# A cap of three gathers in flight in a fused graph layer on one core

## The reference, cut to what matters

```python
# x (12500, 64) f32, src and dst (400000,) int32, dst sorted, edge_attr_64 (400000, 64) f32
msg = x[src] + edge_attr_64
agg = segment_sum(msg, dst, num_segments=12500)
h = relu(agg @ W1 + b1)
x = layernorm(x + h @ W2 + b2, eps=1e-5)
```

## Time and profile before

| what | value |
|---|---|
| median of 3 runs | 2372.08 us |
| profiled execution: its own time | 2373.34 us |
| its span from first to last instruction | 2371.5 us |
| PE busy | 1501.9 us, 63% |
| DVE busy | 1234.8 us, 52% |
| POOL busy | 968.9 us, 41% |
| ACT busy | 738.2 us, 31% |
| gathers (line 610) on POOL | 925, 889.4 us busy |
| mean granted clock of PE | 0.738 |

### The profile page before, as it was taken

How to read it: one execution, slowest core, us unless ns; L and a number is a source line. 1 busy time by engine, 2 the same in 40 slices (tenths; PEclk the granted TensorE clock), 3 DMA queues, 4 the chain that set the end, 5 groups by cost and what they waited for, 6 DMA issues and landing times.

```text
span 2371.5 us, 45768 instructions
## 1 busy us (share of the span) xinstructions
PE 1501.9 (63%) x18752; PEld 1318.1 (56%) x18753; DVE 1234.8 (52%) x2701; ACT 738.2 (31%) x935; POOL 968.9 (41%) x1045
## 2 busy tenths in 40 slices
PE   2555656566657576666566676555756666657776
PEld 1555545455646566656555665455655565546664
DVE  4765545555546355645545554434545554445535
ACT  5322111122223233323222343323433333323323
POOL 7644454443443433443433434343244334243432
PEclk6556776776777767777767777777878777778798
DMA  7322222222212222222222222221222222212232
GB/s 188 75 78 78 76 71 71 61 71 63 79 50 76 68 65 66 69 67 69 69 55 61 73 61 64 54 57 50 69 62 53 61 61 63 59 50 63 69 64 55
DMA packets 150052, 161.03 MB, mean 68 GB/s; under 512 B 42291, under 2 KB 134035, under 8 KB 149507
## 3 DMA queue, kind: packets, MB, share of 16 engines
q1 hardware_dynamic: 118229, 123.61, 18.0%
q0 software_dynamic: 31616, 34.50, 7.5%
HBM read 153.06 MB, written 4.93 MB: 67 GB/s over the span
## 4 chain that ended last, share of the span: by engine, by line
PE 48%; another core or an unknown queue 21%; issue 16%; ACT 8%; DVE 4%; POOL 1%; DMA 1%; DVEq 0%; POOLq 0%; SPq 0%; ACTq 0%
PE sums_ps L1155 18%; PE counted_ps L1138 16%; PE chunk_ps L1120 13%; ACT counts L721 7%; DVE oh_key L937 1%; DVE oh_lo L933 1%; POOL xmsg L610 1%; PE turn_ps L1166 1%; POOL x_parts L659 0%; PE turn_ps L1091 0%; DVE counts L946 0%; DMA lists<-in_src 0%; DMA records<-edge_records,run_at 0%; DVE lists L902 0%
## 5 line engine op out<-in xcount | busy, mean ns | idle before, releaser
L610 POOL DMA_INDIRECT xmsg<-in_x,idx_t x925 | 889.4, 961 | 922.8 <-PE chunk_ps L1120 634.6
L721 ACT CAST counts<-counted_ps 128x784 bf16<-128x784 f32 (+2 forms) x728 | 615.5, 864 | 1385.8 <-remote 667.0
L1138 PE MATMUL counted_ps<-oh_key,oh_lo 128*128 128x98 bf16 (+1 forms) x5264 | 677.8, 257 | 582.1 <-ACT counts L721 335.1
L933 DVE TENSOR_TENSOR oh_lo<-chunk_ps,tables 128x768 bf16<-128x768 f16 (+3 forms) x622 | 446.2, 717 | 764.5 <-remote 359.9
L1138 PEld LDWEIGHTS counted_ps<-oh_key,oh_lo 128*128 128x128 bf16 x5264 | 437.7, 115 | 683.7 <-issue 351.0
L1155 PE MATMUL sums_ps<-x_parts,counts 128*128 128x193 bf16 (+3 forms) x4900 | 749.3, 284 | 56.6 <-issue 55.8
L1155 PEld LDWEIGHTS sums_ps<-x_parts,counts 128*128 128x128 bf16 (+3 forms) x4900 | 542.4, 136 | 74.5 <-issue 64.5
L937 DVE TENSOR_TENSOR oh_key<-chunk_ps,tables 128x1176 bf16<-128x1176 f16 (+2 forms) x622 | 459.9, 739 | 0.0
L1120 PE MATMUL chunk_ps<-onehot,cmsg 128*64 128x16 f32 (+4 forms) x4400 | 227.2, 241 | 116.1 <-issue 115.5
L1120 PEld LDWEIGHTS chunk_ps<-onehot,cmsg 128*64 128x64 f32 x4400 | 206.4, 173 | 146.7 <-issue 141.0
L619 POOL DMA_INDIRECT records<-edge_records,run_at x42 | 39.6, 944 | 394.4 <-DVE run_at L827 371.3
(11 more groups left out here) (111 smaller groups left out, 446.4 us busy)
## 6 DMA issues: line engine op xcount, KB each, us to landing
cmsg<-in_edge_attr SPq DMA_DIRECT2D x440, 160.0 KB
gmsg<-in_edge_attr SPq DMA_DIRECT2D x185, 160.0 KB
xmsg<-in_x,idx_t POOLq DMA_INDIRECT x925
out_nodes<-x_parts SPq DMA_DIRECT2D x11, 256.0 KB, 2.6
edge_records<-counts SPq DMA_DIRECT2D x1, 1500.0 KB
lists<-in_src SPq DMA_DIRECT2D x1, 1400.0 KB
lists<-in_dst SPq DMA_DIRECT2D x1, 1400.0 KB
records<-edge_records,run_at POOLq DMA_INDIRECT x42
```

What stands on the lines that cost most here:

```text
L610: pool.indirect_dma_start(xmsg[:, at * D:(at + 1) * D], None, x, bass.IndirectOffsetOnAxis(ap=idx_t[:, of:of + 1], axis=0)).then_inc(gathe ...
L721: nc.scalar.copy(to.rearrange("p h (m n) -> p h m n", m=m), ps.rearrange("p m (n h) -> p h m n", h=HI)).then_inc(unit_kept, 1)
L933: nc.vector.tensor_tensor(oh_lo[s % RING][:, 0:n * P].rearrange("p (k n o) -> p k n o", k=n, o=2), lo_ps.rearrange("p (n o) -> p n o", o=2 ...
L1138: mm = nc.tensor.matmul(unit_ps[u][:, col:col + slot.key_cols], oh_lo[s % RING][:, n * P:(n + 1) * P], oh_key[s % RING][:, n * slot.key_co ...
```

## The change: three semaphores in turn

Gathers are numbered q = 5k + j through the whole kernel. Gather q waits on POOL until gather q - 3 has landed, and raises semaphore q mod 3. PE waits, for each gathered chunk, on all three semaphores, each for the last of its gathers up to the chunk's end.

```diff
+IN_FLIGHT = 3
...
-        gathered = [sem(f"gathered{s}") for s in range(XSLOTS)]
+        landed = [sem(f"landed{f}") for f in range(IN_FLIGHT)]
...
                 if j == 0 and k >= XSLOTS:
                     pool.wait_ge(summed, PLACE["gather", k - XSLOTS] + 1)
+                q = k * TILES + j
+                if q >= IN_FLIGHT:
+                    pool.wait_ge(landed[q % IN_FLIGHT], 16 * (q // IN_FLIGHT))
                 at, of = t * TILES + j, k * TILES + j
                 pool.indirect_dma_start(xmsg[:, at * D:(at + 1) * D], None, x,
                                         bass.IndirectOffsetOnAxis(ap=idx_t[:, of:of + 1], axis=0)
-                                        ).then_inc(gathered[t], 16)
+                                        ).then_inc(landed[q % IN_FLIGHT], 16)
...
                 pe.wait_ge(gin[s], 16 * (i // GSLOTS + 1))
-                pe.wait_ge(gathered[t], 16 * TILES * (i // XSLOTS + 1))
+                last = i * TILES + TILES - 1
+                for f in range(IN_FLIGHT):
+                    pe.wait_ge(landed[f], 16 * ((last - f) // IN_FLIGHT + 1))
```

## The result

The changed kernel takes **2349.0 us** (median of 4 runs, 2330.4 to 2353.5) against 2372.2 for the kernel before beside it: a ratio of 0.990, with a 95% interval of 0.987 to 0.993. A second comparison gave 0.9905 (0.9875 to 0.9935). The forecast was 2378, no change. The profiled execution is the longest of the four, 2353.5 us; its span is 2351.7.

A forecast was written before the change was run, and what follows sets the result against it. PE was taken to bound the kernel, with POOL's gathers ahead of it except at the start. +4 us (start) and +2 (PE's waits) on the profiled 2373.3 gave 2379.3, or 2378 against the median; range 2362 to 2396.

The forecast's parts named there:

- The reading of the bound: Whole kernel: PE is busiest, 1501.9 of 2371.5 us, and in the long middle the gathers are ahead of it.
- PE's waits: On PE before gathered pairs: 370 more waits, none blocking, cost +2 us, bounds 0 and 18.5.
- POOL's slack: Mid-kernel: POOL waits 1006 us for PE and DVE, so slowing it under 1.09 us per gather costs nothing.
- The start: POOL's first gathers: the cap delays the first records that DVE awaits, +4 us, bounds 0 and +13.6.
- L = 6.0: At the start: assumed us from a gather's beginning to its landing, between quiet 2.4 and 7.70 beside the x load.
- Rival A: At the start: L stays under 4.3, so the change does nothing and only PE's +2 remains, 2374; chance 0.15.
- the quiet landing: Last gather of a burst, with nothing following: from its beginning to its landing at most 2.4 us.
- The wait on POOL: On POOL before 922 gathers: the wait instruction itself, when already met, was priced at 0.
- The middle: Mid-kernel gathers: the cap does not bind, at most two gathers being under way at any moment; no gain or loss.
- The slack under the limit: Mid-kernel: a landing takes at most 2.4 us, 1.4 us under the 3.75 at which the cap would bind.
- Rival C: Mid-kernel: pauses between gathers end PE's slow stretches sooner; two of 14 us gone, -28, with +6 2350; chance 0.10.
- D: Mid-kernel: waits stretch bursts, so PE spends more time beside gathers; two more slow stretches, +28, with +6 2406; chance 0.10.

The follow-up runs named there:

- own_cap_start: `own_sems` with the cap of three for gathers 3 to 24 alone; 2393.6 us, ratio 1.0096 to the kernel before.
- own_sems: Kernel before, no cap, with one semaphore for each of the 25 ring places and 740 more waits on PE; 2381.5 us, ratio 1.0042.
- pe_waits: Kernel before with some 370 more waits on PE, all already met, and no cap; 2370.6 us against 2366.6, ratio 1.0008.
- own_met_wait: `own_sems` with an always-met wait on POOL before each gather from 25 on; 2356.0 us, ratio 1.0037 to the kernel before.
- own_cap_later: `own_sems` with the cap of three for gathers from 25 on alone; 2338.1 us, ratio 0.9848 to the kernel before.
- own_cap2_later: `own_cap_later` with a cap of two in place of three; 1929.9 us, ratio 0.8212 to the kernel before (slow kind).
- late_cap: The changed kernel with its first 25 gathers left free of the cap; 2310.1 us, ratio 0.9834 to the kernel before (slow kind).
- memset_between: Kernel before with a POOL memset after every second gather from 25 on, its wait always met; 1393.5 us, ratio 1.0002 (quick kind).

## Why the prediction was wrong

**The reading of the bound held.** PE's waits and POOL's slack were what the rows said, and on this kind of chip 22 to 29 us of added idle on POOL cost nothing.

**The start: right mechanism, term too small.** Forecast +4 us with bounds 0 and 13.6; measured +11.0 in the profile (9.7 without the late first gather) and +12 by `own_cap_start` less `own_sems`. The failed number is L = 6.0. I had argued that two DMAs ahead instead of five would shorten 7.70; the landings took 12.9, 9.2 and 7.9 us, 10.0 on average, though only three of them, not four, stood in a row. They were long while the x load filled the engines, which the cap does not shorten, and the waits ended with it: of the two arguments beside the 6.0 the one for a short L was wrong. Rival A falls too. The rule of the Trainium skill weighed there ("DMA: Bandwidth & Descriptors", "Anatomy of one DMA — SWDGE (gpsimd) path"), about 2.0 us fixed, agrees with the quiet landing, at most 2.4 us, and not with these.

**PE's waits: +2 us, in agreement** with `pe_waits` (1.0008, -2 to +6 us). The wait on POOL at 0: confirmed by `own_met_wait`.

**The middle: the step that failed** is "In the middle the cap does not bind", with what hung on it, "what slows POOL by less than 1.09 us per gather costs nothing". Two errors are in it. First, not every gather of a burst lands as soon as the lone one that I took my L from, and between a landing and the start that it releases POOL needs time of its own, 0.26 us in the chain of the start. The slack under the limit, put at 1.4 us, was too small for the scatter: 54 gathers of the kernel after stood still, by 0.4 us on average. The pause of 1.34 us above means a landing 4.5 us after its gather began (3.75, plus 1.34 less 0.30, less 0.26). By itself this error is small. Second, and this turned the sign, a pause on POOL was taken to cost nothing and so to bring nothing. On this kind of chip it brings: 43 us for 28.8 us of added idle in `own_cap_later`.

**Rival C was the right one**, at a chance of 0.10, with its link and its sign. That its 2350 lies within 1 us of the 2349.0 measured is luck: it took -28 for two whole stretches of 14 us that are gone and +6 for the rest, where the runs give about -43 for many small gains and +14 for the start and PE's waits. I held it back for one reason, that the cap would have to bind where I said it does not. The evidence for its other half stood in the earlier trace rows, and I gave too little weight to 37% of the chain being unexplained. Its condition, "where landings take over 3.75 us within a burst", was a little too strict, since a landing must also come some 0.3 us before the start that it releases. D, the same link with the other sign, is refuted on this kind of chip: with gathers further apart PE's slow stretches are shorter.

**What stays open.** Shown: pauses of tenths of a microsecond between gathers shorten the kernel on one kind of chip, by 1.0 to 1.7 us for each us of pause, and the large one, the cap of two, shortens PE's unexplained idle; a met wait, a wait instruction as such or the semaphores do not. Not shown: what couples POOL's gathers to PE's progress there, whether a pause has to be a wait for a landing to bring the 18% of the cap of two, and in what the two kinds of chip differ. Nor can the trace tell whether PE's work itself is late or only the signal of its end, since the ends of matmuls are modelled, and ACT and DVE, which wait for such signals, have long unexplained waits as well. That PE is held by POOL's bursts is read from the 58 of 65 long idle stretches that lie in one, and agrees with every run on the slow kind; half of those stretches end before the burst does, and a run that takes away the gathers and leaves PE's work was not made. `own_cap2_later`, at 0.82, is faster than both kernels on the slow kind, and `late_cap` is 1.7% faster than the kernel before. Neither is advised where the kernel may meet a quick chip: there a cap of two lost 21% and the change itself 3.5%, and `late_cap` was not run. No version that ran on both kinds beat the kernel before on both.

## What to carry to other kernels

Where a large share of the chain is "issue" or an unknown queue, look at what the other engines are doing in those very microseconds before calling one of them slack: an engine that has time to spare may still hold up the one that has none. Take the duration for "does it bind?" from the crowd in which the instruction will run, with the time from release to start added, and not from the one instance that stands alone. And time a change on more than one chip before keeping it: the same cap changed the time by -1% on one kind and by +3.5% on the other, where the profile shows that POOL's slack is gone. And take off the idle that every instruction of a group has before summing "its waits": of the 36.1 us that ended with a landing in `own_cap_later` only 12.0 were a pause (the rest of its 28.8 us stood under "issue").

## What the runs showed of the hardware

- The same program took 2348 to 2372 us on some chips and 1393 us on others. DVE and ACT were busy for nearly the same time (1211 and 739 us in `memset_between` against 1235 and 738 in the kernel before), PE for 1199 instead of 1502 us at a higher granted clock (0.923 against 0.738).
- On the slow kind PE, and at times ACT and DVE, stood still for up to 11.9 us without a visible cause, mostly while POOL issued gathers 1.25 us apart (58 of 65 idle stretches of over 3 us), and went on at the burst's end or within it. Added idle of 28.8 us between gathers gave back 1.9% (`own_cap_later` against `own_sems`), 281 us (a cap of two) 18%.
- An indirect DMA took at most 2.4 us from issue to landing when alone, up to 4.5 us within a burst of the kernel after, and 7.7 to 12.9 us beside a bulk load that filled the DMA engines.
- A wait that is already met cost nothing measurable ahead of an indirect DMA on POOL, and some 13 to 20 ns on PE (740 of them, 10 to 15 us).
